# Ten of the first item's twenty maxima in the second self attention are taken in the projection stage ahead of it

## The reference

```python
h = _layernorm(x, ln1_w, ln1_b)
qkv = (h @ qkv_w + qkv_b).reshape(B, T, 3, H, HD)
q, k, v = [qkv[:, :, i].transpose(0, 2, 1, 3) for i in range(3)]
attn = jnp.einsum('bhtd,bhsd->bhts', q, k) * scale
attn = jnp.where(causal[None, None], neg, attn)
attn = jnp.where(tgt_mask[:, None, None, :], neg, attn)
attn = jax.nn.softmax(attn, axis=-1)
sa = jnp.einsum('bhts,bhsd->bhtd', attn, v).transpose(0, 2, 1, 3).reshape(B, T, C)
x = x + sa @ proj_w + proj_b
```

## Time and profile before

| what | value |
| --- | --- |
| time, median of 3 runs | 1787.26 us (1785.79 to 1788.02) |
| profiled execution: time | 1787.46 us |
| profiled execution: span | 1785.7 us |
| mean granted TensorE clock | 0.975 of full speed |
| PE busy | 1633.4 us (91%) |
| DVE busy | 1141.7 us (64%) |
| ACT busy | 1060.8 us (59%) |
| POOL busy | 962.2 us (54%) |

### The profile page before, as it was taken

The page is one execution under the profiler, slowest core; times in us unless marked ns, Lnnn a source line. Parts: engine busy times, 40 slices in busy tenths (PEclk is TensorE's granted clock), DMA queues, the critical chain, the costliest instruction groups (busy, mean ns, idle before and its releaser), DMA issues. The chain is left out here.

```text
span 1785.7 us, 28486 instructions
## 1 busy us (share of the span) xinstructions
PE 1633.4 (91%) x9748; PEld 1046.9 (59%) x9748; DVE 1141.7 (64%) x1985; ACT 1060.8 (59%) x1376; POOL 962.2 (54%) x734
## 2 busy tenths in 40 slices
PE   6889999999999999988998989996989888898799
PEld 4445545444444444378787978884445436565579
DVE  7557677777777777476775933347787845776513
ACT  4556688888888888833556433311767772454452
POOL 1456688888888888952233710202334444566405
PEclk9999999999999999999999999995999999999899
DMA  3011021111111111030000010103234321000101
GB/s 98 24 34 33 36 69 37 43 35 41 53 47 35 41 35 36 24 107 27 1 2 13 1 39 24 25 13 90 55 85 96 73 74 31 9 1 2 36 15 48
DMA packets 54312, 70.92 MB, mean 40 GB/s; under 512 B 18176, under 2 KB 41884, under 8 KB 54207
## 3 DMA queue, kind: packets, MB, share of 16 engines
q1 hardware_dynamic: 54207, 69.54, 14.0%
HBM read 41.72 MB, written 2.37 MB: 25 GB/s over the span
## 5 line engine op out<-in xcount | busy, mean ns | idle before, releaser
L1694 POOL TENSOR_TENSOR x<-x,sa_p_buf 128x1024 f32<-128x1024 f32 x190 | 453.5, 2387 | 126.9 <-ACT sa_p_buf L1430 114.1
L1562 DVE TENSOR_REDUCE sa_mx<-sa_front 128x1 f32<-128x512 f32 x512 | 327.7, 682 | 106.4 <-PE sa_front L1285 105.4
L1430 ACT ACTIVATE sa_p_buf<-sa_score 128x1024 f32<-128x1024 f32 x256 | 249.2, 1023 | 130.6 <-PE sa_score L1322 130.4
L1341 PE MATMUL sa_out<-sa_p_buf,sa_v_buf 128*64 128x512 f32 x1024 | 246.4, 602 | 0.0
L607 ACT ACTIVATE sa_p_buf<-sa_score 128x1024 f32<-128x1024 f32 (+1 forms) x160 | 140.6, 942 | 74.6 <-PE sa_score L555 74.5
L402 DVE TENSOR_REDUCE sa_mx<-sa_front 128x1 f32<-128x512 f32 (+1 forms) x224 | 136.5, 651 | 31.8 <-PE sa_front L316 28.3
L2686 POOL TENSOR_TENSOR x<-x,bias_out 128x1024 f32<-128x1024 f32 x24 | 61.3, 2570 | 168.8 <-POOLq L3014 142.0
L1285 PE MATMUL sa_front<-sa_k_hi,sa_q_hi 64*128 64x512 f32 x512 | 116.8, 452 | 22.2 <-DVE sa_mx L1562 17.1
L1341 PEld LDWEIGHTS sa_out<-sa_p_buf,sa_v_buf 128*64 128x64 f32 x1024 | 64.5, 136 | 123.6 <-issue 97.5
L1440 ACT ACTIVATE sa_score<-sa_m_all 128x1024 f32<-128x1024 f32 x128 | 130.9, 1035 | 0.5 <-DMA sa_m_all<-sa_m_line 0.5
L660 POOL TENSOR_SCALAR_AFFINE_SELECT sa_p_buf<-sa_p_buf 128x128 f32<-128x128 f32 x256 | 65.6, 293 | 119.2 <-ACT sa_p_buf L607 119.2
(11 more groups left out here) (284 smaller groups left out, 3526.7 us busy)
## 6 DMA issues: line engine op xcount, KB each, us to landing
sa_m_all<-sa_m_line SPq DMA_DIRECT2D x16, 512.0 KB, 3.7
x<-sa_m_line SPq DMA_DIRECT2D x16, 512.0 KB, 4.4
sa_v_buf<-o SPq DMA_DIRECT2D x15, 512.0 KB, 5.1
x<-in_x SPq DMA_DIRECT2D x8, 512.0 KB, 5.5
sa_q_stack<-sa_hi SPq DMA_DIRECT2D x32, 128.0 KB, 2.6
sa_k_stack<-sa_hi SPq DMA_DIRECT2D x32, 128.0 KB, 2.7
sa_recip<-sa_den_out SPq DMA_DIRECT2D x32, 128.0 KB, 2.7
ff_w<-in_L_xattn_ff_w SPq DMA_DIRECT2D x16, 128.0 KB, 2.1
```

The source lines that it names most:

```text
L1341: mm = pe.matmul(out_ps[64 * j:64 * j + 64, :], v_buf[:, b, kt, 64 * j:64 * j + 64], p_buf[:, s % NPB, j, :], start=(kt == 0), stop=(kt == ...
L1430: nc.scalar.activation(p_buf[:, s % NPB], score_ps[s % len(score_ps)][:], ACT.Exp, scale=SCALE).then_inc(exp_done, G)
L1562: dve.tensor_reduce(mx[:, b, j, qt, half:half + 1], front_ps[bank(item, j)][:], AX.X, ALU.max).then_inc(drained, 1)
L1694: nc.gpsimd.tensor_tensor(acc[:, h], prev, cur, ALU.add).then_inc(added, 1)
```

## The change

Ten maxima of item 0 are put into the slots 6 to 9 of `early`: three, two, two and three. In each slot they alternate with the p and the v, beginning with a maximum. They use the `front` banks there, and have a reduction for each head. The other ten stay in `late` and keep the scores' banks (`borrowers`).

```diff
--- before.py
+++ after.py
@@ -137,7 +137,16 @@
     for n in range(TT // GROUP):
         b, part = divmod(n, NPROJ)
         early[n + 2] += [(b, ("p", part)), (0, ("v", n))]
-    late = [(0, m) for m in maxima] + [(0, ("t",))] + [(1, m) for m in maxima[:EARLY]]
+    COUNT = {6: 3, 7: 2, 8: 2, 9: 3}
+    EARLIEST = sum(COUNT.values())
+    coming = iter(maxima[:EARLIEST])
+    for n, count in COUNT.items():
+        mixed = [(0, next(coming)) for _ in range(count)]
+        for at, item in zip((1, 3), early[n]):
+            mixed.insert(at, item)
+        early[n] = mixed
+    borrowers = maxima[EARLIEST:]
+    late = [(0, m) for m in borrowers] + [(0, ("t",))] + [(1, m) for m in maxima[:EARLY]]
     assert sum(item[0] == "v" for slot in early + [late] for _, item in slot) == 2 * NPROJ
 
     def width(item):
@@ -145,7 +154,7 @@
 
     def borrowed(i, item):
 
-        return i == 0 and item[0] == "m"
+        return i == 0 and item in borrowers
 
     def by_pool(i, item):
 
@@ -262,9 +271,9 @@
     def wait_bank(pe, i, item, k):
 
         if borrowed(i, item):
-            n = maxima.index(item)
+            n = borrowers.index(item)
             if k == 0 and n >= PAIRS:
-                pe.wait_ge(drained, DRAINED[i, maxima[n - PAIRS], 1])
+                pe.wait_ge(drained, DRAINED[i, borrowers[n - PAIRS], 1])
         elif FREE[i, item, k] is not None:
             of, prior, _ = FREE[i, item, k]
             if by_pool(of, prior):
@@ -274,7 +283,7 @@
 
     def bank(i, item, k=0):
         if borrowed(i, item):
-            return score_ps[maxima.index(item) % PAIRS][:, k]
+            return score_ps[borrowers.index(item) % PAIRS][:, k]
         return front_ps[PLACE[i, item, k] % NBANK]
 
     def made(pe, i, item):
@@ -387,7 +396,7 @@
             qt, k0, n = top[f][0]
             place = qt if k0 == 0 else qt + 4
             if borrowed(i, item):
-                both = score_ps[maxima.index(item) % PAIRS]
+                both = score_ps[borrowers.index(item) % PAIRS]
                 dve.wait_ge(front_full, filled(i, item, 1))
                 if segs == 1:
                     dve.tensor_reduce(mx[:, b, 2 * r:2 * r + 2, place], both[:, :, 0:n], AX.X, ALU.max).then_inc(drained, 2)
```

## The result

The changed kernel takes 1797.14 us (median of 10 runs, 1792.04 to 1806.66), the kernel before 1787.64 (10 runs, 1785.79 to 1790.03). The ratio is 1.0052, with a 95% interval of 1.0036 to 1.0068: slower by 0.5%. The time lies inside the range of 1787 to 1799, the sign was forecast with 0.68, and the forecast of 1792.6 is 4.5 us too low. The runs of the changed kernel scatter over 15 us and those of before over 4 in this comparison, but the kernel before scatters over 6, 12 and 9 us in the 19, 30 and 17 runs beside the experiments (a further one, of 3004.86 us at a granted clock of 0.864, is left out of every ratio).

A forecast was written before the change was run, and what follows sets the result against it. The change moves work from a prologue that DVE bounds to a projection stage that PE bounds: 13.1 of waits, less 9.5 given back, plus 1.7 for the clock, gives +5.3 us, forecast median 1792.6, range 1787 to 1799.

The forecast's parts named there:

- the sign: Whole kernel: slower by more than 0.2%, or 3.6 us, chance 0.68; faster by more than that 0.09, within 0.23.
- Slot 6: Projection stage: M1 waits for its transfers, M2 for M1's reductions behind the normalisation; the slot ends 4.4 us later.
- Slots 7 and 8: Projection stage: M4's pair and P's reading stand behind the normalisation; 9.5 us in place of 6.48, 3.0 more in slot 7.
- Slot 9: Projection stage's end: V waits for P's bank, 1.3 us more; M10's pair on DVE adds 1.3 until the boundary.
- the stage's 13.1: Slots 6 to 9: waits for DVE's reads make the prologue begin 13.1 us later, the clock's part not included.
- The prologue: To the first scores: ten fewer reductions save 10.8 us, of which 9.5 are given back; scores 22.8 after the first matmul.
- The wait for SP's queue: Prologue: of the 10.8 us removed, 1.3 turn into a wait for SP's queue ahead of the first scores.
- the 18.8 us that I gave to SP: Prologue: SP's time issuing transfers without a wait, from 1211.40 to 1230.20, ahead of the turned maxima's four.
- the rival with SP not late: Prologue gives back all 10.8 us; with the clock held +2.3, 1789.6 us; chance 0.12.
- The clock: Slots 6 to 9: PE's new waits cause one fall to 1.2 GHz, costing 1.7 us.
- my rival at 1796.0: Clock falls in three slots, 6, 7 and 8, costing 5.1 us; +8.7 in all; chance 0.15.
- The likeliest case: Whole kernel: one fall of the clock, 1790.5 to 1794.5 us, chance 0.42.

The follow-up runs named there:

- added twice: Changed kernel, but the prologue still does all twenty maxima, so ten are done twice; against the kernel before: 1808.32 us, ratio 1.0123.
- fillers that fit: Changed kernel plus unread matmuls of the gaps' length in slots 6 to 9; against the kernel before: 1792.3 us, ratio 1.0034.
- masks moved: Changed kernel plus the gap-length unread matmuls, eight small mask transfers issued from ScalarE's queue; against the kernel before: 1792.95 us, ratio 1.0031.
- too many fillers: Changed kernel plus unread matmuls in slots 6 to 9 that took longer than the waits; against the kernel before: 1801.55 us, ratio 1.0097.
- maxima read first: Changed kernel, VectorE reading first maximum and P ahead of the residual sum in slots 6 to 8; against the kernel before: 1790.96 us, ratio 1.0020.

## Why the prediction was right, and where it was short

- **What bounds the stretches.** Right. Ten maxima that VectorE has time for cost a stage that PE bounds 13 us and give one that VectorE bounds 10 back.
- **Slot 6.** Forecast +4.4. The waits ahead of M1 (0.82) and M2 (1.64) came as worked out. From turn to product it was 8.38 in place of 3.03, so +5.35. The clock is at 0.50 from 1198.20 to the product at 1200.15, and half of these 1.95 us is its part; +4.4 remain. V starts 0.15 behind VectorE's reading of P, as said, but M2 fills the time ahead of it, so no wait shows there.
- **Slots 7 and 8.** Right: the wait ahead of M5 and M7 stands behind the statistics and the pair of M4 and M6. Slot 8, all of it at full clock, takes 9.45 from its product at 1212.09 to the next turn at 1221.54, and 9.5 was the sum.
- **Slot 9.** Right: V waits 0.75 for P's bank, and the boundary waits for M10's pair. Without the clock's part the stage's 13.1 is borne out by four profiled executions: 12.9 (changed), 13.1 (added twice), 13.2 (fillers that fit) and 13.2 (masks moved, where M1 starts 1.35 behind the turn and the clock is at 1.00).
- **The prologue.** Right: -9.5 forecast, -9.7 in the trace, and the scores 22.56 us behind the first matmul where 22.8 was said. The wait for SP's queue was 1.26 for 1.3, and 0 to 1.2 in other kernels. That it fits so closely is luck: the 18.8 us that I gave to SP held a hold-up of 1.3 us, as the rival with SP not late had it (17.6 without one), the changed kernel's execution had one of 0.9 of its own, and from the last issue to the scores it took 1.28 to 2.40 us. (My terms there add up to 22.7, not 22.8.)
- **The clock.** This is the term that was mis-sized: "So I expect one fall", +1.7. The profiled run has three, 5.05 together, the upper end and my rival at 1796.0, which I had given 0.15; it had them in slots 6, 7 and 8, and they came in 6, 7 and 9. Against the kernel with fitting fillers the clock costs 4.7 us in the two profiled stages, 4.8 by the medians, and 3.2 by the ratios, which is not clear of the noise. I had counted the fall once because slot 6 had the longest standing; but the clock also fell behind the wait of 1.69 in slot 7 and those of 0.52 and 0.75 in slot 9, and not behind the 1.91 in slot 8, where it fell in another execution.
- **The Trainium skill** (TensorE: Matmul & The Clock Gate, section "Why this matters for your kernels") names only long idle gaps between bursts as what loses the clock. The traces here disagree: no gap in slots 6 to 9 was longer than 1.91 us, and the clock fell three times. What the reader can use is the row of 1213.85 in the earlier trace rows, which was in the profile before the change.
- **What is left.** 13.1 - 9.7 + 5.05 gives 8.4; the profiled run has 8.0, with 1.3 that it was late ahead of slot 6 already and 1.5 that it won back behind the scores. Falls of the clock in code that the change leaves alone may account for both: from 972 to 981 us the mean clock was 0.62 after and 1.00 before, from 1494 to 1500 it was 0.50 before and 1.00 after. The medians differ by 9.5, 1.5 more than the two profiled runs. The runs of the changed kernel go with their mean granted clock: the five up to 1795.45 us have 0.975 to 0.978, the five from 1798.84 have 0.966 to 0.973. So the 1.5 go with the clock, but whether they belong to the new waits or to falls elsewhere stays open, since only one of the ten runs has a trace.

The likeliest case, one fall, had been given 1790.5 to 1794.5, and the median lies 2.6 above it. The measured time lies in the range because the range had room for three falls, not because the likeliest case came.

## What to carry to other kernels

Before work is put into the gaps of an idle engine, look at what stands in order ahead of its reader there: VectorE was less than half busy, and M1, M4 and M6 still waited for a statistics chain of 2.4 us. Moving the reads ahead of that chain is not enough: it moved the waits. What added none were two maxima placed directly behind the product and one in a gap that TensorE had already. Whether more than three `front` banks would do it for ten was not run. When the receiving stage is one that TensorE bounds, price the waits twice, once for their length and once for the clock behind each of them, and allow for a fall behind every such wait; two and three came here behind four of them. A stretch that runs at half clock because TensorE idles in small pieces can be cheaper to fill with matmuls that nobody reads (2.7 us gained here) than to empty of work (9.5 us lost).

## What the runs showed of the hardware

- A wait of 1.6 to 1.9 us between matmuls at full load may or may not be followed by a stretch of about 3.4 us at half clock; two kernels with the same three waits, equal to a hundredth of a us, fell in different slots, three times and twice.
- The time of a run goes with its mean granted clock, in the kernel before too: its 30 runs beside the second group of experiments reach from 1781.77 us at 0.979 to 1793.73 at 0.971. A large scatter is therefore no sign of the new waits: the kernel without the ten maxima scatters over 12 us (1775.77 to 1787.50), the one with too many fillers over 15, the one with fitting fillers over 10 and the one with maxima read first over 6.
- The clock also falls for a few us at a time outside these stages, and at other places in another execution (0.50 from 1494 to 1500 us in the kernel before, 1.00 there in the changed one).
- One call of a 128x128 by 128x256 matmul in this 32-bit form is recorded as two matmuls and took 0.45 us (3.62 for eight calls), so counts of matmuls in a profile are not counts of calls.
